# First layer of a two-layer graph network: high and low value products merged for even row blocks, h recomputed, x1 written late

## What is computed

```python
h = jnp.maximum(_layernorm(x, axis=-1), 0.0)
wh = h @ W
e = wh @ a[:F_OUT, :] + (wh @ a[F_OUT:, :]).T
e = jnp.where(e > 0, e, ALPHA * e)
e = jnp.where(adj > 0, e, NEG_BIG)
x = x + jax.nn.elu(jax.nn.softmax(e, axis=-1) @ wh)
h = jnp.maximum(_layernorm(x, axis=-1), 0.0)
Qn, Kn = _cos_normalize(h @ Wq.T), _cos_normalize(h @ Wk.T)
att = jax.nn.softmax(jnp.where(adj > 0, Kn @ Qn.T, NEG), axis=1)
x = x + 0.5 * (att @ h) + 0.5 * h
```

## Time and profile before

| | before |
|---|---|
| median of 3 runs | 2189.89 us |
| the profiled execution | 2189.39 us |
| its span, first to last instruction | 2187.6 us |
| TensorE busy in the span | 2142.1 us, 98% |
| VectorE busy | 1963.5 us, 90% |
| ScalarE busy | 1752.8 us, 80% |
| layer 0's matmuls begin | 54.35 us |
| chunk 7 of layer 0 ends | 774.5 us |
| scores of layer 1 begin | 810.1 us |

### The profile page before, as it was taken

How to read it: one execution, slowest core, us unless ns; L and a number is a source line. 1 busy time by engine, 2 the same in 40 slices (tenths; PEclk the granted TensorE clock), 3 DMA queues, 4 the chain that set the end, 5 groups by cost and what they waited for, 6 DMA issues and landing times.

```text
span 2187.6 us, 63203 instructions
## 1 busy us (share of the span) xinstructions
PE 2142.1 (98%) x26185; PEld 1733.5 (79%) x26185; DVE 1963.5 (90%) x1686; ACT 1752.8 (80%) x1928; POOL 33.0 (2%) x43
## 2 busy tenths in 40 slices
PE   5999999999999979999999999999999999999998
PEld 5999999999999956777777777777777777777776
DVE  7999999999999858889888898898898898898987
ACT  6687778878788668888888888888888888888886
POOL 1000000000000030000000000000000000000000
PEclk9999999999999989999999999999999999999999
DMA  6899999999999916565565665665665666656653
GB/s 248 328 382 401 390 405 397 401 402 399 403 400 388 361 40 217 193 223 204 207 215 196 224 212 196 220 220 193 214 221 200 212 204 216 215 194 218 218 193 115
DMA packets 153732, 573.52 MB, mean 262 GB/s; under 512 B 9936, under 2 KB 10576, under 8 KB 153168
## 3 DMA queue, kind: packets, MB, share of 16 engines
q1 hardware_dynamic: 142176, 546.02, 68.3%
q10 hardware_dynamic: 11376, 24.91, 3.0%
HBM read 558.24 MB, written 12.65 MB: 261 GB/s over the span
## 4 chain that ended last, share of the span: by engine, by line
PE 95%; DVE 2%; ACT 1%; issue 1%; DMA 0%; POOL 0%; ACTq 0%; POOLq 0%; DVEq 0%
PE bank L1197 32%; PE bank L1245 30%; PE bank L1266 21%; PE bank L1261 10%; DVE hl_buf L726 1%; PE bank L1152 1%; PE bank L1172 0%; DVE hl_buf L714 0%; DMA ring<-adj 0%; ACT hl_buf L558 0%; ACT ring L619 0%; POOL hl_buf L401 0%; PE bank L1094 0%; PE bank L1134 0%; DMA q_buf<-x 0%
## 5 line engine op out<-in xcount | busy, mean ns | idle before, releaser
L619 ACT ACTIVATE ring<-bank,th_col 128x512 f32<-128x512 f32 x1024 | 647.1, 683 | 231.0 <-PE bank L1245 223.3
L988 DVE SCALAR_TENSOR_TENSOR ring<-ring 128x2048 f32<-128x2048 int32 x256 | 586.4, 2291 | 154.5 <-ACT ring L619 154.5
L1197 PE MATMUL bank<-v_buf,ring 128*128 128x129 f16 (+1 forms) x12288 | 711.9, 220 | 6.3 <-DVE ring L902 6.1
L1197 PEld LDWEIGHTS bank<-v_buf,ring 128*128 128x128 f16 x12288 | 707.8, 98 | 9.8 <-issue 8.9
L1245 PE MATMUL bank<-v_buf,q_buf 128*128 128x512 f16 x3072 | 706.4, 380 | 5.2 <-ACT ring L619 5.2
L1266 PE MATMUL bank<-u_buf,hl_buf 128*128 (+1 forms) x8192 | 704.3, 220 | 0.0
L1266 PEld LDWEIGHTS bank<-u_buf,hl_buf 128*128 128x128 f16 x8192 | 631.8, 98 | 55.9
L902 DVE SCALAR_TENSOR_TENSOR ring<-r_ring,th_word,ring 128x1024 f32<-128x1024 f32 x512 | 619.3, 1277 | 19.3 <-ACT ring L448 19.1
L993 DVE TENSOR_TENSOR hl_buf<-ring,hl_buf 128x2048 f16<-128x2048 f32 x256 | 584.5, 2284 | 0.0
L1261 PE MATMUL bank<-u_buf,hl_buf 128*128 (+1 forms) x2048 | 557.9, 272 | 0.5 <-DVE hl_buf L993 0.5
L448 ACT ACTIVATE ring<-ring 128x2048 f32<-128x2048 int32 x256 | 481.2, 1908 | 88.4 <-DMA ring<-adj 85.0
(11 more groups left out here) (138 smaller groups left out, 433.0 us busy)
## 6 DMA issues: line engine op xcount, KB each, us to landing
ring<-adj SPq DMA_DIRECT2D x512, 1024.0 KB, 5.6
r_ring<-a_rows SPq DMA_DIRECT2D x8, 512.0 KB, 7.0
x_dram<-q_buf ACTq DMA_DIRECT2D x8, 512.0 KB, 7.2
h_dram<-hl_buf ACTq DMA_DIRECT2D x8, 512.0 KB, 7.4
r_ring<-x_dram ACTq DMA_DIRECT2D x16, 256.0 KB, 4.2
r_ring<-h_dram ACTq DMA_DIRECT2D x16, 256.0 KB, 4.4
out<-r_ring ACTq DMA_DIRECT2D x16, 256.0 KB, 4.8
r_ring<-k_rows ACTq DMA_DIRECT2D x15, 256.0 KB, 4.1
```

The costliest lines, as they stand in the source:

```text
L619: ins = nc.scalar.activation(p_ring[:, k, (2 * hf + m) * IW:(2 * hf + m + 1) * IW], bank[:, 2 * hf + m, :], ACT.Exp, scale=q_scale[:, j:j ...
L988: V.scalar_tensor_tensor(p_ring[:, k, :], adj_ring[:, k, :], 0.0, p_ring[:, k, :], ALU.is_gt, ALU.mult).then_inc(s_m, 1)
L1197: ins = mm(acc0(par, it), weights0(k, ps)[:, it // 4, jj, f], v2[:, bass.ds((2 * j + us) * VW, D + 1)], start=False, stop=False, skip_grou ...
```

## The change

In layer 0 an even row block makes high by high and high by low with one matmul of 259 columns (WIDE), so a unit has 40 matmuls. The low part of an even block's sums then lies beside the high part and is added in the epilogue. The sums take 4 banks per parity, that is all 8, so the banks of the transition move. VectorE's `denominators` becomes two copies, an addition and a reciprocal; its `negative` no longer takes a minimum but adds the low parts with four instructions out of PSUM; ScalarE makes the negative part with a Relu before the exponential. The preset moves from `quotient` to `exponential` and clears the columns between, too. The high copy of h moves from VectorE to ScalarE.

h is no longer written to DRAM and read back: the scale and bias of all rows are kept, and ScalarE computes h again in layer 1 (`residual_h`). x1 of chunks 0, 4 and 7 is written as before by ScalarE's queue, that of chunks 1, 5, 2, 6 and 3 by SyncE's queue behind the last load of layer 0. `sizes` moves from chunk 1 to chunk 0.

```diff
+WIDE = VW + D + 1
+X1_EARLY = (0, 4, 7)
+X1_LATE = (1, 5, 2, 6, 3)
...
         def acc0(par, it):
-            b, k = 3 * par + it // 3, it % 3
-            return bank[:, b, k * (D + 1):(k + 1) * (D + 1)]
+            k = it % 2
+            return bank[:, 4 * par + it // 2, k * WIDE:k * WIDE + D + 1]
...
             chunks0(chunk)
+            for c in X1_LATE:
+                sp.wait_ge(s_ev, len(EPI0) * c + EPI0.index("x1") + 1)
+                sp.dma_start(x1_dram[:, c * C0:(c + 1) * C0], xs[:, c * C0:(c + 1) * C0]).then_inc(s_x1w[c % (NC0 // 2)], 16)
...
             def preset(par):
-                for i in range(3):
-                    g = acc0_group(par, i)
-                    ins = nc.scalar.activation(g, v_sum[:, :].unsqueeze(1).to_broadcast([P, g.shape[1], D + 1]),
+                sums = bank[:, 4 * par:4 * par + 4, 0:WIDE + D + 1]
+                nc.scalar.activation(sums[:, :, D + 1:WIDE].rearrange("p b (s n) -> p b s n", s=2),
+                                     ident[:, 0:D // 2 + 1].unsqueeze(1).unsqueeze(1).to_broadcast([P, 4, 2, D // 2 + 1]),
+                                     ACT.Copy, scale=0.0)
+                for k in range(2):
+                    ins = nc.scalar.activation(sums[:, :, k * WIDE:k * WIDE + D + 1],
+                                               v_sum[:, :].unsqueeze(1).to_broadcast([P, 4, D + 1]),
                                                ACT.Copy, scale=EMPTY)
...
-                    if not (isinstance(c, int) and c == NC0 - 1):
-                        act.wait_ge(s_free, c + 1)
-                        act.nop(nofuse=True)
-                        preset(par)
...
                 def exponential():
-                    act.wait_ge(s_ev, at("neg"))
-                    nc.scalar.activation(e_buf, e_buf, ACT.Exp).then_inc(s_ea, 1)
+                    act.wait_ge(s_ev, at("low"))
+                    nc.scalar.activation(e_buf, z_buf, ACT.Relu, scale=-1.0).then_inc(s_neg, 1)
+                    act.wait_ge(s_neg, c + 1)
+                    nc.scalar.activation(e_buf, e_buf, ACT.Exp, scale=-1.0).then_inc(s_ea, 1)
+                    if c != NC0 - 1:
+                        preset(par)
...
                 def root():
-                    act.wait_ge(s_ev, at("x1"))
-                    act.dma_start(x1_dram[:, bass.ds(c * C0, C0)], xs[:, bass.ds(c * C0, C0)]).then_inc(s_x1w, 16)
+                    if c in X1_EARLY:
+                        act.wait_ge(s_ev, at("x1"))
+                        act.dma_start(x1_dram[:, bass.ds(c * C0, C0)], xs[:, bass.ds(c * C0, C0)]).then_inc(
+                            s_x1w[c % (NC0 // 2)], 16)
...
                     act.wait_ge(s_ea, 3 * c + 3)
-                    act.dma_start(h_dram[:, bass.ds(c * C0, C0)], h_buf).then_inc(s_hw, 16)
+                    nc.scalar.activation(u_buf[:, bass.ds(c * IT0, IT0), 0:D], h_buf.rearrange("p (t f) -> p t f", f=D),
+                                         ACT.Copy).then_inc(s_uh, 1)
...
             def copy_ht(g):
+                act.wait_ge(s_x1w[g // 4], 32)
...
-                act.dma_start(e_h, h_dram[:, bass.ds(i * IW, IW)]).then_inc(s_fin, 16)
+            def residual_h(i):
+                act.wait_ge(s_fin, 16 * (i + 1))
+                for it in range(IT1):
+                    f, t = slice(it * P, (it + 1) * P), i * IT1 + it
+                    ins = nc.scalar.activation(e_h[:, f], e_x1[:, f], ACT.Relu, bias=nbias[:, t:t + 1], scale=rstd[:, t:t + 1])
+                ins.then_inc(s_eh, 1)
...
-                    parts = {(0, 2): lambda: key_high(i + 1), (1, 1): quotient, (2, 1): store, (2, 2): lambda: residual(i),
+                    parts = {(0, 2): lambda: key_high(i + 1), (1, 1): quotient, (2, 1): store, (2, 2): lambda: residual(i), (3, 2): lambda: residual_h(i),
...
                 def denominators():
                     dve.wait_ge(s_used, U0 * (c + 1))
-                    for b in range(3):
-                        g = acc0_group(par, b)
-                        ins = V.reciprocal(den[:, 0, 3 * b:3 * b + g.shape[1]], g[:, :, D])
-                    ins.then_inc(s_ev, 1)
+                    V.tensor_copy(den[:, 1, 1:IT0:2], acc0_column(par, WIDE + D))
+                    V.tensor_copy(den[:, 2, 0:IT0:2], acc0_column(par, VW + D)).then_inc(s_ev, 1)
+                    dve.wait_ge(s_ev, at("densum"))
+                    V.tensor_tensor(den[:, 1, 0:IT0:2], acc0_column(par, D), den[:, 2, 0:IT0:2], ALU.add).then_inc(s_ds, 1)
+                    dve.wait_ge(s_ds, c + 1)
+                    V.reciprocal(den[:, 0, :], den[:, 1, :]).then_inc(s_ev, 1)
...
                 def negative():
                     dve.wait_ge(s_free, c + 1)
-                    V.tensor_scalar(e_buf, z_buf, 0.0, None, ALU.min).then_inc(s_ev, 1)
+                    for it in range(0, IT0, 2):
+                        f = slice(it * P, (it + 1) * P)
+                        ins = V.scalar_tensor_tensor(z_buf[:, f], acc0_wide(par, it)[:, VW:VW + D], den[:, 0, it:it + 1],
+                                                     z_buf[:, f], ALU.mult, ALU.add)
+                    ins.then_inc(s_ev, 1)
...
-                    V.tensor_copy(hi, h8).then_inc(s_ev, 1)
-                    dve.wait_ge(s_ev, at("hi"))
+                    dve.wait_ge(s_uh, c + 1)
                     V.tensor_tensor(u_buf[:, bass.ds(c * IT0, IT0), D + 2:UW], h8, hi, ALU.subtract).then_inc(s_ev, 1)
...
                 elif g == EARLY + 1:
                     pe.wait_ge(s_rr, 1)
-                    pe.wait_ge(s_free, NC0)
+                    pe.wait_ge(s_ev, len(EPI0) * (NC0 - 1) + EPI0.index("low") + 1)
...
-                                for ps, us in parts:
+                                if it % 2 == 0:
+                                    mm(acc0_wide(par, it), weights0(k, 0)[:, it // 4, jj, f],
+                                       v2[:, bass.ds(2 * j * VW, WIDE)], start=False, stop=False, skip_group_check=True)
+                                for ps, us in parts[2:] if it % 2 == 0 else parts:
```

More of the change, by code:

```diff
@@ L529, in chunk, with second_set @@
                     parts = {2 * (q - ZR) + 2: (lambda q=q: value_high(q)) for q in range(ZR, T // ZT)}
-                    parts[25] = lambda: preset(1)
+                    def second_set():
+                        act.wait_ge(s_wsum, 2)
+                        preset(1)
+                    parts[23] = sizes
+                    parts[25] = second_set
                     value_high(0)
@@ L957, in _ @@
             denominators()
+            negative()
             copy_rows(0)
[L959 removed]
             copy_ht(7)
```

65 lines of the change are left out of this document (32 added, 33 removed).

## The result

| | before | after |
|---|---|---|
| median of 6 runs each, us | 2190.63 (2189.19 to 2192.54) | 2204.81 (2200.77 to 2211.78) |
| ratio, 95% interval | | 1.0065 [1.0055, 1.0075] |
| profiled execution, us (span) | 2189.4 (2187.6) | 2204.2 (2202.4) |
| layer 0 ends, us from the span's start (its last matmul's start and 0.06) | 774.3 | 786.2 |
| end of layer 0 to the first scores, us | 35.8 | 38.5 |

The kernel became slower by 0.65%. Of the 14.8 us between the spans 11.9 are in layer 0, 2.7 in the transition and 0.3 in layer 1.

The account below looks back on a forecast made before the run. TensorE bounds the kernel, but each layer 0 chunk's epilogue is a loop through DMA, ScalarE and VectorE with 1 us to spare. 2189.4 + 7.5 (layer 0) + 2.3 (transition) = 2199.2; median 0.5 above, 2199.7 us, range 2194.5 to 2205.

Parts of the forecast that it names:

- The pace of TensorE: Layer 0 units: 2.707 us instead of 2.755, 0.048 less, which makes 1.55 us a chunk.
- The stalls: Layer 0, chunks 2 to 6: TensorE waits at units 12, 18 and 20, 2.9 us lost a chunk against 1.55 gained.
- Unit 18's stall of 0.2: Layer 0, ahead of unit 18: the copy of h on ScalarE uses up VectorE's lead, so TensorE waits 0.2 us.
- The lead at unit 10: Layer 0, end of unit 10's weights on VectorE to its matmuls' start: falls from 5.6 to 2.4 us.
- Chunk 7: Layer 0's last chunk: no row factors loaded ahead of unit 8, masks about 1 us sooner, so only +0.35 us.
- is not relieved: VectorE, chunks 1 to 7: minimum and cast go, four PSUM instructions and longer denominators come, in sum +0.3 us.
- Relu costs table loads: Rival, ScalarE in layer 0: Relu needs another table, 1.28 us more in each of 7 parts, 2208.7 us; chance 0.06.
- DMA relief: Layer 0: 1 MB less of x1 and h writes in most chunks, taken as 0 for the lead at units 10 to 12.
- The transition: End of layer 0 to layer 1: later denominators, exponential and copy of h, one load issue gone; +2.3 us (0.5 to 4).
- Layer 1: Recomputing h on ScalarE, four instructions, 1.6 us, fits in without TensorE waiting; cost 0.
- the merge pays in full: Rival, layer 0: the lead at unit 12 stays positive, so faster matmuls count in full, -8.8 us, 2181.1 us; chance 0.24.

Follow-up runs that it names:

- the version with all moves: Changed kernel with preset behind unit 24, copy of h behind unit 19 (chunk 7's on VectorE), row factors ahead of unit 24's load, x1 writes later: 2187.18 us.

## Why the prediction held, and where its terms were off

The forecast was 2199.7 us, and 2204.81 was measured (runs of 2200.77 to 2211.78): the sign and the mechanism held, the sum was 5 us too low. Against the profiled execution I had +9.8 and it is +14.8.

*The pace of TensorE* was mis-sized. The step "16 more columns at the granted 2.4 GHz add 0.007: 2.707 us a unit" took the unit from layer 1's value part in the earlier trace rows, by subtracting the scores' modelled time from a distance between two starts. Measured are 2.718 us (86.97 us for 32 units in the version with all moves) against 2.754 before (88.12 us), so 0.036 less and not 0.048. That is 0.4 us a chunk, 2 to 3 us of the missing 5.

By the Trainium skill (TensorE: Matmul & The Clock Gate, "Wait — 56ns, not 53.3ns?") a matmul costs its columns and 2.5 ns, and the prediction made 0.037 of it, which looks like a hit. It is luck. A unit loses 8 matmuls (48 to 40) and not the 16 that were put in; with 8 the Trainium skill's figure gives 8 x 2.5 ns less 3.3 ns for the 8 columns more, an estimate of 0.017 us, half of what was measured. Here each matmul taken away was worth 4.9 ns, (36 + 3.3) / 8, though a matmul costs only 3.6 ns besides its columns on average before (57.4 less 53.75) and 3.4 after. Why the ones taken away were worth more than the average no run shows.

*The stalls* were sized almost right. With the pace as measured, each chunk gains 1.15 us; chunks 2 to 6 are longer by 2.0, 3.3, 2.0, 1.0 and 1.2, so TensorE lost 3.2, 4.5, 3.1, 2.1 and 2.3 in them, 3.0 on average (0.3 of it by the clock, see below) for the 2.9 predicted. The average hides that no chunk is like another, and by the profile of the version with x1's writes later the order of the chunks isn't a property of the kernel. The place was right too: units 10 to 12 and 20. Unit 18's stall of 0.2 didn't come (lead 0.25). ScalarE's part behind unit 9 grew by 2.6 us, predicted 2.8; the preset took 1.58 (438.43 to 440.01), predicted 1.65. The lead at unit 10 was forecast at 2.4 and lies between 1.2 and 3.5. What I had as one number for all chunks varies: the load of unit 8 or 9 lands 8.5 to 9.0 us after TensorE has finished the unit that frees its slot in chunks 2 to 4, 7.7 to 7.9 in chunk 5, 6.2 to 6.4 in chunk 7. Chunks 4 and 5 do the same work but for a write of x1, which is chunk 5's, and chunk 5 is the shorter one by 1.05 us; in the profile of the version with the later writes it is the longer one, by 2.2, and the granted clock fell in it.

The stalls have a second price, which I had put at nothing without a word: the granted clock. In chunk 3 TensorE stood for 2.2 us ahead of unit 12, and behind that the clock fell to half for part of unit 12, which took 4.42 us for 2.72. In chunk 4 TensorE stood as long and the clock held:

```profile
363.00:368.00 5.00, 5.00 (x49) 4.52 (x50) 5.00 (x5) 4.88 (x3) 0.00 (x0) 0.66 0.64 242
454.00:459.00 5.00, 4.62 (x68) 4.44 (x69) 5.00 (x6) 5.00 (x3) 0.00 (x0) 1.00 0.72 257
```

Chunk 3 is 1.3 us longer than chunk 4 by it (1.7 lost at unit 12, 0.4 of it won back, since VectorE was then ahead at unit 20). Such a fall goes with long waits, and not with each: in layer 0 of the profiles there is none before, none in the versions of 2195 us and less, and one to three in each of the others (in chunks 2 to 6 at unit 11 or 12, in chunk 7 in three of them in the long unit 26). No run sets such a wait by itself.

*Chunk 7* was the second mis-sized term: +0.35 forecast, +1.9 measured. Its waits ahead of units 12 and 20 cost 1.2 us, less than the 1.9 I had; but units 26 and 27 take 5.68 and 5.77 us for 5.06 and 4.69 before, 1.7 more together. There TensorE waits with the first query and key products for the copies of the transposes, ahead of unit 27 for ScalarE's, which stands behind its last mask (1.04), and ahead of unit 28 for VectorE's (1.12), so a late load can show up twice. I had not read that wait in the trace of before, where it was 0.38. The wait ahead of unit 27 in after, in the timeline:

```profile
764.24 1.48 PE L1179 MATMUL bank<-wqk_sb,q_buf 128*128 128x256 f16 x12 [1.04 <-ACT q_buf L569]
```

*VectorE* "is not relieved": 1963.5 and 1962.6 us busy. *Relu costs table loads*: no; one table load stands in the part behind unit 9, ahead of the exponential, none at the Relu. *DMA relief* was taken as 0: in the version with all moves, x1's half of it given back changes nothing. h's half wasn't tried by itself.

*The transition* was forecast at +2.3 and is +2.7. The quotient comes 0.36 later, and the exponential 1.9 later against the end of layer 0 (forecast +2.0), behind Relu and the low parts:

```profile
786.83 0.20 DVE L845 RECIPROCAL den<-den 128x8 f32<-128x8 f32 x1
...
789.27 1.13 DVE L851 SCALAR_TENSOR_TENSOR hl_buf<-bank,den,hl_buf 128x128 f32<-128x128 f32 x4 [2.24 <-ACT hl_buf L501]
...
790.43 1.06 ACT L507 ACTIVATE hl_buf<-hl_buf 128x1024 f32<-128x1024 f32 x1 [0.28 <-DVE hl_buf L851]
...
791.33 2.67 PE L1179 MATMUL bank<-wqk_sb,q_buf 128*128 128x256 f16 x12 [0.42 <-DVE hl_buf L961]
791.52 1.06 ACT L509 ACTIVATE hl_buf<-hl_buf 128x1024 f32<-128x1024 f32 x1
```

The square root is then 2.0 later, the first of the last four groups of products (815.99 us) 2.4 and the last two (822.00) 2.7. *Layer 1* was forecast at 0 and is +0.3; `residual_h` fits in behind its unit. Its four Relus, 1.64 us at L667, push nothing that can be seen in the time of the layer:

```profile
989.60 1.64 ACT L667 ACTIVATE r_ring<-r_ring,nbias,rstd 128x128 f32<-128x128 f32 x4
```

*The rival "the merge pays in full"* decides from a lead over 0 at unit 12, and the changed kernel has 0.18 there in chunks 1 to 6 and 0.06 in chunk 7: TensorE waits for it. Once the preset, the copy of h and the row factors are out of the way the lead is there in chunks 4 to 7 (0.5 to 1.5 us; still 0.18 in 1 to 3) and the rival comes true in these, though not in the total: 6.3 us of the 9.2.

What stays open: why unit 31's load in chunk 7 lands late in some variants (5.4 to 9.0 us after its issue), which goes with a unit 26 of between 5.7 and 10.1 us; why the transition is 37.9 to 39.8 us in the variants whose edits don't reach it, and up to 41.1 in the others; and how much of the spread of after's runs, 11 us where before spreads over 3.4, is the clock. The slowest of the six, 2211.78 us, has a mean granted clock of 0.989 and the fastest, 2200.77, one of 0.992, so it has a part in it, of at most 7 us by an estimate (0.003 of 2212). That a lead near 0 also lets every late load through to TensorE fits, and the version with the lead restored spreads over 5.5 us, but this was only argued.

## What to carry to other kernels

In a ring loop (consumer frees, DMA, first engine, second engine, consumer) the quantity to read is the lead of each unit, from the end of its preparation to the start of its use, unit by unit and not as a share of busy time: 1 us on ScalarE cost 4.6 us in six chunks at the thinnest place and 1.5 a dozen units later. Work that isn't due until later (a preset for the next chunk, a copy of a result) is put where the lead is largest, and a faster matmul shortens each lead as well (at unit 12 of chunk 4, with all moves, 2.3 us with narrow matmuls and 1.5 with wide ones), so it has to come together with such a move. When an operation changes engines, ask which of the two is queued in front of the next unit, not which is busier. And a wait of some 2 us of TensorE may cost more than itself, as in chunk 3: 1.3 us on top.
